# A layer of state-space mixing, cross-attention and experts on one core: an addition moved to GpSimd, roots and small products issued earlier, head biases in fp16, and products that nobody reads put into waits of TensorE

## What is computed

```python
# 1: two small Mamba blocks (forward, backward), each on half of the width
xn = rmsnorm(x);  out = concat(mamba(xn[:, :64]), flip(mamba(flip(xn[:, 64:])))) @ op_w.T + op_b
x = layernorm(x + (x + out))
# 2: cross-attention; queries from x, keys and values from the context AND from x
ln, cn = layernorm(x) * g_l + b_l, layernorm(ctx) * g_m + b_m
q = ln @ Wq + bq                      # 8 heads of 128
k, v = split(concat(cn, ln) @ Wkv + bkv)
x = layernorm(x + softmax(q k.T / sqrt(128)) v @ Wo + bo)
# 3: 8 experts, the best 2 of each row, and a shared one
x = layernorm(x + sum(weight_e * swiglu_e(xn)) + shared(xn))
```

## Time and profile before

| | us |
|---|---|
| time, median of 3 runs | 1834.78 |
| lowest and highest | 1833.75, 1834.96 |
| the profiled execution: its own time | 1832.03 |
| its span, first to last instruction | 1830.2 |
| PE busy | 1756.0 (96%) |
| DVE busy | 1499.0 (82%) |
| ACT busy | 1123.8 (61%) |
| POOL busy | 258.3 (14%) |
| mean granted clock of TensorE | 0.982 of full speed |

### The profile page before, as it was taken

One profiled execution on the slowest core, in us unless ns is written; L12 is line 12 of the kernel. 1 busy time (PEld: TensorE's weight loads), 2 busy tenths in 40 slices (PEclk: granted clock), 3 DMA queues, 4 the chain that ended last, 5 costly groups with the idle time before them and its releaser, 6 DMA issues.

```text
span 1830.2 us, 31285 instructions
## 1 busy us (share of the span) xinstructions
PE 1756.0 (96%) x9183; PEld 874.8 (48%) x9183; DVE 1499.0 (82%) x2397; ACT 1123.8 (61%) x1375; POOL 258.3 (14%) x323
## 2 busy tenths in 40 slices
PE   5987899999999999999999999999999999999998
PEld 3764344444444444444444444444444444444665
DVE  7677898888797879797979787888788888756987
ACT  4453566666666666656666666566666666676665
POOL 2832796000000000000000000000000000000554
PEclk8978999999999999999999999999999999999999
DMA  4001110000000000000000000000000000000000
GB/s 142 2 1 35 35 57 17 1 0 0 0 0 0 0 0 0 0 0 0 0 0 0 0 0 0 0 0 0 0 0 0 0 0 1 0 0 1 1 7 7
DMA packets 15380, 14.08 MB, mean 8 GB/s; under 512 B 5855, under 2 KB 13795, under 8 KB 14950
## 3 DMA queue, kind: packets, MB, share of 16 engines
q1 hardware_dynamic: 15334, 13.49, 2.4%
HBM read 12.96 MB, written 0.52 MB: 7 GB/s over the span
## 4 chain that ended last, share of the span: by engine, by line
issue 80%; POOL 10%; PE 7%; DVE 2%; ACT 1%; POOLq 0%; DMA 0%; SPq 0%; DVEq 0%; ACTq 0%
PE PS L1521 6%; POOL z_arena L587 4%; POOL w_arena L582 2%; POOL w_arena L578 2%; POOL w_arena L580 2%; DVE w_arena L960 0%; DVE mxs L1380 0%; ACT z_arena L742 0%; POOL w_arena L502 0%; PE PS L1530 0%; DVE w_arena L969 0%; DMA vecs<-in_L_attn_b_conv_w 0%; SPq L343 0%; ACT ah_arena L733 0%; ACT AH L732 0%
## 5 line engine op out<-in xcount | busy, mean ns | idle before, releaser
L792 ACT ACTIVATE p_arena<-PS 128x1024 f16<-128x1024 f32 (+1 forms) x480 | 484.8, 1010 | 523.6 <-PE PS L1521 523.4
L1521 PE MATMUL PS<-a_arena,z_arena 128*128 (+1 forms) x2832 | 746.7, 380 | 1.2 <-DVE a_arena L1209 1.2
L1521 PE MATMUL PS<-p_arena,z_arena 128*128 128x512 f16 x2800 | 740.4, 379 | 1.4 <-ACT p_arena L802 0.3
L1222 DVE TENSOR_TENSOR p_arena<-p_arena 128x1024 f16<-128x1024 f32 (+1 forms) x480 | 575.3, 1198 | 109.2 <-ACT p_arena L795 98.6
L1190 DVE TENSOR_REDUCE mxs<-PS 128x512 f32 (+1 forms) x900 | 581.8, 667 | 86.9 <-PE PS L1521 83.6
L795 ACT ACTIVATE p_arena<-PS 128x1024 f32<-128x1024 f32 (+1 forms) x480 | 481.5, 1003 | 0.0
L1521 PEld LDWEIGHTS PS<-a_arena,z_arena 128*128 (+1 forms) x2832 | 275.0, 98 | 329.3 <-issue 1.9
L1521 PEld LDWEIGHTS PS<-p_arena,z_arena 128*128 (+1 forms) x2800 | 269.3, 98 | 312.3 <-ACT p_arena L802 8.8
L1521 PE MATMUL PS<-z_arena,a_arena 128*128 (+3 forms) x1024 | 353.6, 361 | 9.9 <-DVE mxs L1190 8.7
L587 POOL TENSOR_TENSOR z_arena<-z_arena 128x512 f16<-128x512 f32 x66 | 76.5, 1160 | 1438.2 <-ACT z_arena L865 1438.0
L1521 PEld LDWEIGHTS PS<-z_arena,a_arena 128*128 (+1 forms) x1024 | 98.2, 98 | 141.9 <-DVE mxs L1190 25.5
(11 more groups left out here) (266 smaller groups left out, 941.5 us busy)
## 6 DMA issues: line engine op xcount, KB each, us to landing
w_arena<-in_L_ffn_gate_up_w SPq DMA_DIRECT2D x8, 512.0 KB, 3.6
p_arena<-in_ctx SPq DMA_DIRECT2D x2, 1600.0 KB, 9.1
w_arena<-in_L_ffn_down_w SPq DMA_DIRECT2D x8, 256.0 KB, 3.9
a_arena<-in_L_xattn_Wkv SPq DMA_DIRECT2D x1, 1024.0 KB, 6.2
w_arena<-in_x SPq DMA_DIRECT2D x1, 512.0 KB, 4.1
a_arena<-in_L_xattn_Wo SPq DMA_DIRECT2D x1, 512.0 KB, 7.0
w_arena<-in_L_xattn_Wq SPq DMA_DIRECT2D x1, 512.0 KB
out<-m_arena SPq DMA_DIRECT2D x4, 64.0 KB, 1.6
```

Source lines behind the costliest of these rows:

```text
L792: s.activation(Phi[:, r % 3, 0:w], ps, ACT.Exp, scale=1 / SSC).then_inc(hi_ready, 1)
L1222: v.tensor_tensor(Plo[:, r % 3, at:w], P32[:, r % 2, at:w], Phi[:, r % 3, at:w], ALU.subtract).then_inc(lo_ready, 1)
L1521: return t.matmul(o, l, r, start=start, stop=stop)
```

## The change

Nothing is changed in the attention blocks and in the expert part, but for one wait. What is changed, by place:

- **Start.** The head biases become fp16: POOL multiplies `brow` by 64, casts it to rows 0 to 2 of `b16` and puts what the cast lost in rows 32 to 34; `bsel` has 35 rows and carries 1/64. A bias product is then one fp16 product with 35 rows in place of a float32 one with 3. The triangular products go from behind convolve(5) to behind convolve(3), and the two products `ow x opT` from behind convolve(2) to behind convolve(1).
- **Context roots.** The 50 chunks are handled in two halves. Statistics, aggregation and root of the first 25 stand ahead of the loop; those of the others go into the loop: 13 statistics behind chunk 0, 12 and the remainder behind chunk 1, aggregation and root behind chunk 2. POOL scales each half when its root is there.
- **Loop.** convolve(8) and (9) are issued ahead of the loop (AHEAD = 2, banks 7 and 6), so that chunks 0 to 2 have two convolutions each and chunk 3 none. The last chunk leaves out the state that nobody needs.
- **Behind the loop.** `keys` 0 and 1 come ahead of `project_out(7)`; in BEHIND_LOOP the root of the row statistics stands behind `keys` 4, the latents ahead of `keys` 8.
- **Output bias.** `acc + boB` is taken from DVE and given to POOL, behind its last score matrix and ahead of the expert weights; DVE waits for it behind block 0.
- **Products nobody reads.** `spin(bank, n, rows)` issues n fp16 products of 128x128 by 128x512 into a bank that is free there: 10 ahead of `rows(0)`; 3 ahead of and 4 behind `project_out(7)`; 6 ahead of the latents; 5 ahead of `a_side(0)`; 4 ahead of the first pair; 8 ahead of and 8 behind `max_to_row(0)` (there behind `combined(7)`). They are 48 products.

```diff
+        AHEAD = 2
-            return (1, 2, 3, 4, 5, 6, 7, 1)[n] if n < 8 else 7
+            return (1, 2, 3, 4, 5, 6, 7, 1, 7, 6)[n] if n < 8 + AHEAD else 7
...
+            pool.wait_ge(ld_b, 48)
+            g.tensor_scalar(brow[0:3, :], brow[0:3, :], BS, None, ALU.mult).then_inc(brow_ready, 1)
+            pool.wait_ge(brow_ready, 1)
+            g.tensor_copy(b16[0:3, :], brow[0:3, :]).then_inc(brow_ready, 1)
+            pool.wait_ge(brow_ready, 2)
+            g.tensor_tensor(b16[32:35, :], brow[0:3, :], b16[0:3, :], ALU.subtract).then_inc(brow_ready, 1)
...
             pool.wait_ge(acc_ready, 1)
+            g.tensor_tensor(acc[:], acc[:], boB[:].unsqueeze(1).to_broadcast([P, TC, D]), ALU.add).then_inc(acc_ready, 1)
...
-            dve.wait_ge(acc_ready, 1)
-            settle(v.tensor_tensor(acc[:], acc[:], boB[:].unsqueeze(1).to_broadcast([P, TC, D]), ALU.add))
...
             block_dve(0, first=True)
+            dve.wait_ge(acc_ready, 2)
...
-            ctx_stats(CC // 2, CC)
+            ctx_aggr(0, CC // 2)
+            for piece in range(5):
+                ctx_root(0, CC // 2, piece)
...
+                if c == 0:
+                    dve.wait_ge(ld_ctx[1], 16)
+                    ctx_stats(CC // 2, CC // 2 + 13)
+                elif c == 1:
+                    dve.wait_ge(ld_ctx[2], 16)
+                    ctx_stats(CC // 2 + 13, CC)
+                    settle(v.bn_stats(st6[0:LEFT, CC, :], ctxl[:]))
+                elif c == 2:
+                    ctx_aggr(CC // 2, CC)
+                    settle(v.bn_aggr(mv[0:LEFT, CC, :], st6[0:LEFT, CC, :]))
+                    for piece in range(5):
+                        ctx_root(CC // 2, CC + 1, piece)
...
-                    mm(b0[:, 0:1], brow[0:3, hs], bsel[:, 0:1], start=False)
+                    mm(b0[:, 0:1], b16[:, hs], bsel[:, 0:1], start=False)
...
+            def spin(bank, n, rows):
+                for _ in range(n):
+                    mm(PS[:, bank, :], I16[:], rows)
+            pe.wait_ge(silu_done, 3)
+            spin(STATE, 10, xTh[:, 0, 0:QB])
...
             turn_gate(TC - 1)
+            for i in range(2):
+                turned_high(i)
+            z_rows = Zhi[:, CTX0:CTX0 + 4, :].rearrange("p c n -> p (c n)")
+            pe.wait_ge(silu_done, 16)
+            spin(7, 3, z_rows)
             project_out(TC - 1)
+            spin(7, 4, z_rows)
...
+                elif kind == "latents":
+                    pe.wait_ge(ah_sb, 4)
+                    spin(7, 6, z_rows)
+                    latents_pe()
...
+            spin(7, 5, z_rows)
             pe.wait_ge(zlT_a, 2)
...
+            spin(0, 4, z_rows)
             pe.wait_ge(a_hi, 2)
...
+            pe.wait_ge(mx_read, NU - 4)
+            spin(0, 8, z_rows)
             max_to_row(0)
             pe.wait_ge(a_lo, 4)
             combined(H - 1)
+            spin(0, 8, z_rows)
             block_pe(0, first=True)
```

More of the change, by code:

```diff
@@ L212, in layer @@
         take = carve(w_arena)
-        Wq, brow, opb = take([H * D]), take([H * D]), take([D])
+        Wq, opb = take([H * D]), take([D])
+        b16 = take([H * D], F16)[0:35]
         x_sb = take([TC, D])
@@ L1586, in convolve @@
                 last.then_inc(conv_ps, 1)
-            for n in range(3):
+            for n in range(2):
                 convolve(n)
@@ L1594, in _ @@
                 mm(PS[:, 7, (1 + q) * P:(2 + q) * P], ow[r, :], opT[r, :]).then_inc(op_ps, 1)
-            for n in range(3, 6):
-                convolve(n)
+            convolve(2)
+            convolve(3)
             pe.wait_ge(dt_v, 2)
@@ L1601, in _ @@
             last.then_inc(tri_ps, 1)
+            convolve(4)
+            convolve(5)
             pe.wait_ge(op_sb, 3)
-            for n in range(6, 8):
+            for n in range(6, 8 + AHEAD):
                 convolve(n)
```

191 lines of the change are left out of this document (106 added, 85 removed).

## The result

The changed kernel took **1826.51 us** (median of 6 runs, 1824.59 to 1828.14), the kernel before 1833.72 beside it (6 runs, 1831.74 to 1834.96). The ratio is 0.9959, with an interval of 0.9946 to 0.9972: faster, by 7.2 us where 18.7 were forecast, and above the range, which ended at 1824. The profiled execution took 1824.59 us with a span of 1822.9.

The account below looks back on a forecast made before the run. In the first 192 us no engine was the bound for long; short steps hand over to each other. 17.7 + 1.4 - 0.4 = 18.7 us off the median 1834.78 gave 1816.1, range 1809.5 to 1824.

Parts of the forecast that it names:

- 1, ahead of the loop: Ahead of the loop: two convolutions and ten unread products move `rows(0)` from 45.75 to 48.7, 3.0 us later.
- the 47.3 case: Ahead of the loop: `rows(0)` would start at 47.3 if PE ran at the full clock throughout.
- 2 and 3, the loop: Chunks 0 to 7: `mixing(3)` at 75.5, 1.7 us later; loop end at 100.5, 4.1 earlier; chunk 0 and 1 statistics cost nothing.
- 4, to `zl`: Behind the loop: DVE's 4.94 us wait for the second root becomes 0.35; `zl` ready at 117.4, 8.9 us earlier.
- 5, to `a_side(0)`: From `zl` to `a_side(0)`: PE and ACT are late next; start at 121.0 to 122.9, taken as 122.0, 9.2 us earlier.
- 6, the bias: Bias addition moved off DVE: `projected(3, 0)` at 130.1, 13.1 us earlier; 1.4 to 1.6 on POOL, up to 9.51; loss 0.4.
- The chain of 8.1 us: From `a_side(0)` to `projected(3, 0)`: the operations left without DVE's bias addition, summed to 8.1 us instead of 11.9.
- 7, the heads: Heads 3 to 6: fp16 bias products at 0.05 us; 8.0, then 5.87 per head, 25.6 for 30.2; 17.7 earlier at pair 17.
- 8, into block 0: From pair 17 into block 0: nothing changes up to 187.51; first products at full clock gain 1.4 us with what follows.
- the 1.4 of the sum: Head of block 0: gain if the clock stays up, six products taking 1.3 instead of 2.6 us, with what follows.
- The chances: Whole kernel: faster 0.93, same 0.04, slower 0.03; the forecast case itself 0.52.
- my rivals: Whole kernel: clock up everywhere 0.15, clock low at the spins 0.15, loop or bias gain missing 0.11, slower 0.03.

Follow-up runs that it names:

- experiments 1: Changed kernel with DVE's normalisation of `acc` moved later, four rows behind the maximum of pair 1 and four behind that of pair 13: 1820.81 us.
- 5: Changed kernel with POOL waiting for its own previous operation ahead of each of the string's subtractions: 1822.97 us, ratio 0.9933.
- experiment 7b: Kernel of experiment 2 with the statistics of chunks 0 and 1 moved ahead of the loop: 1815.59 us.
- experiment 2: Changed kernel with one wait added ahead of POOL's cast, so that DVE ends its normalisation of `acc` first: 1816.09 us, ratio 0.9905.
- 7a: Kernel of experiment 2 without the ten unread products ahead of `rows(0)` and the six ahead of the latents: 1815.69 us.
- 6 on POOL's wait: Kernel of experiment 2 without any of the 48 products that nobody reads: 1816.51 us.

## Why the prediction was wrong

**1, ahead of the loop: right in kind, off by 1.8 us.** I took convolve(8)'s six products at the low clock of the trace before; they ran at the full one, which I had named as the 47.3 case (46.91). That was luck as much as reason: `rows(0)` of two other executions with the ten (experiments 1 and 5) started at 49.61 and 49.38, with the clock at 0.72 in 42 to 48.

**2 and 3, the loop: right.** `mixing(3)` at 75.17 for 75.5, the loop's end at 99.98 for 100.5; the statistics are covered by PE, as experiment 7b shows.

**4, to `zl`: right.** 117.40 for 117.4, a wait of 0.38 us for the second root.

**5, to `a_side(0)`: this step failed.** It asked what is late next, and named PE and ACT. It went from `zl` being ready straight to the turning and the low parts, and left out the eight rows of `acc` that DVE does in between. They cost nothing as long as they take 2.13 us, or even the 2.56 of experiment 2, where DVE waited 0.90 for ACT behind them. But step 4 moved them 8.9 us up, POOL's cast and string moved 10.3 (128.85 to 118.56), and so the string starts while the fifth of the rows is standing and three are still to do. Its sum should have had POOL's chain laid out beside DVE's: cast at 118.6, string at 120.1, end at 129.3, and on DVE rows from 117.4 on. Everything for it stood in the rows: an operation of DVE beside the string takes until its end. I had this rule for the addition and did not ask of which other operation of DVE it would now be true. It cost 9.45 us at `a_side(0)` (131.45 for 122.0), 10.4 by the distance in experiment 2, where `a_side(0)` came at 122.89, inside the 121.0 to 122.9 of this step.

**6, the bias: right where the stand is gone, and mis-sized on POOL.** With POOL's wait it is worth 3.4 us. The chain of 8.1 us became 10.85 after and 9.49 in experiment 2, mostly since after the change four unread products and the first pair took 1.89 and 1.82 us at the low clock, not 0.87 and 0.43. On POOL the addition took 2.35 us, not 1.6. I had 1.37 per 896 columns from a group of three with 4.11 us; but in the order of instructions these are two of 896 columns and one of 128, and the two take 1.84 each like all others. My "1.84 next to DVE, 1.37 alone" was a mean over two shapes, so the agreement of the rows that I read out of this pair is none; what the rows do show is DVE's addition at 9.51. By 1.84 the estimate would have been 2.1. And this false pair of prices had me believe that the string loses by the collision; it does not, only DVE does there. In the end POOL's 2.35 us cost nothing that the traces show, as DVE waits for ACT 3.53 us in that place.

**7, the heads: right.** 25.74 for 25.6: 7.62 for the first, where I had 8.0, and 6.04 for each of the others, where I had 5.87. The two errors nearly cancel. The fp16 bias product costs 0.10, not 0.05:

```profile
142.69 0.17 PE L1559 MATMUL PS<-bsel,w_arena 35*128 35x1 f16 x1
142.79 0.70 PE L1559 MATMUL PS<-Tm,a_arena 128*128 128x256 f32 x2
```

It starts at 142.69, what follows at 142.79.

**8, into block 0: right.** 17.86 from pair 17 on for 18.4, and the clock at 1.00 in the nine products, 2.12 us for 3.95; 2.0 us in all for the 1.4 of the sum.

With the hold taken away the kernel stands at 1816.09, and 1816.1 was forecast. That it fits to the digit is luck: the four runs go from 1813.86 to 1821.52, and the profiled one took 1816.35 where the sum gave 1813.3. By the markers 1.9 of these 3.0 us are missing at the scores of block 0 (175.98 for 174.1), since `projected(3, 0)` came 2.3 late. The sum of the parts that I did name, 18.7, was thus some 3 too high by the trace, and right in kind. The chances were wrong all the same. None of my rivals was a new meeting of two engines, although I wrote that "nothing to be seen" would need a new wait of 10 us and that I saw no place for one. There was one of 9.3.

## What to carry to other kernels

When a chain moves up, list on each engine what stood beside it and what stands beside it now: the collision that one operation had is inherited by the next one that shares the engine, and a fix made for the first (the addition to POOL) buys nothing until the second is out of the way. A stand of 9.5 us on an operation that takes 1.2 alone is a reason to look for all operations of that engine within reach of the same partner, and often one wait, which lets the short side finish first, is worth more than moving work. Filler products are to be tried group by group: the ten in front of a step that was ready cost 2.2 us, the sixteen ahead of block 0 went with 0.9 less in both pairs of traces, and the nine around `a_side(0)` with 0.55 less or 2.15 more, by the clock that they met. A filler that ends behind the release of the next step costs what it is late, and at the low clock it is twice as long.

## What the runs showed of the hardware

A DVE operation from SBUF to SBUF that met POOL's string stood until POOL waited for something, not until the current operation ended. The fifth row of `acc`, of one float32 input, lasted 9.72 us beside POOL's L577 (0.47) and five subtractions of 1.84 that follow with no wait between them in POOL's code. With a wait ahead of each subtraction the rows took at most 2.04, one for each. POOL's cast has a wait on either side of it, and the row beside it was out when the cast was: 118.61 to 119.74 for 118.56 to 119.66, though POOL's records leave no gap there. That it is the wait in the code that lets DVE in is read from these few rows. The Trainium skill, SBUF — State Buffer, section "SBUF: two separate sides", says that whichever starts first has the shared ports for its whole instruction. Beside operations with waits between them the trace agrees (1.95 and 1.96 from row to row for POOL operations of 1.88); without waits a string counted as one instruction, and the measurement decides.

The string loses nothing by it, 9.21 to 9.24 us in all traces. But POOL is not always the one that wins. Ahead of block 0 a DVE operation from SBUF to SBUF started first, and POOL's, which takes 0.67 alone, stood beside it (the trace after):

```profile
184.63 1.21 DVE L1246 TENSOR_TENSOR a_arena<-R,a_arena 1x1024 f16<-1x1024 f32 x1
```

```profile
184.78 1.60 POOL L568 TENSOR_TENSOR ah_arena<-AH,ah_arena 128x256 f16<-128x256 f32 x1 [16.83 <-ACT ah_arena L759]
```

DVE operations with one input in PSUM are not held: both low parts of the latents ended 1.29 us after the first began at 121.50 in experiment 2, across the start of the string at 122.06, and the maxima kept their 1.23.

POOL adds two float32 operands of 128x1024 in 2.35 us, DVE alone in 1.21, 1.94 times as fast. The Trainium skill, GPSIMD Engine Reference, section 4.1, has about two; the traces agree.

The clock ahead of the loop is not the same in all executions of the changed kernel and its variants: 1.00 in 42 to 48 in some, 0.72 in others, with `rows(0)` 2 to 3 us later. The four with 0.72 (experiments 1, 5, 7a and 6 on POOL's wait) already had 0.67 to 0.72 in 28 to 36, the others 0.73 to 0.85. Nothing in which these variants differ lies ahead of 41 us. It is the likeliest source of the spread of up to 8 us within the runs of one kernel, but only the profiled execution of each can be read, so this is argued and not shown.
